# A language-model block on one core: shared down product with stationary weights, experts' first blocks fixed at the end, two gathers in flight

## Chip, cores and metric

One core of one Trainium2 chip. The metric is the device time of one execution, in microseconds, of this core.

## The reference

2048 tokens (4 sequences of 512) of width 128. Three steps, of which the third is the one that the change touches:

```python
h = take(W.T, x)                                       # embedding rows, 2048 x 128
h = h + ssm_attention(layernorm(h))                    # s = tanh(s @ A.T + x_t @ B.T), gated, projected
x = layernorm(h)
logits = x @ gate_w.T                                  # 8 experts, top 1
y = silu(x @ w1[e].T) * (x @ w3[e].T) @ w2[e].T        # e = the token's expert, inner width 512
y = y + gelu(x @ sw1.T) @ sw2.T                        # the shared expert, for every token
out = h + y
```

With one expert taken, its softmax weight is 1.

## The kernel before

**Until the experts.** The recurrence runs as 32 chunks of 16 steps side by side, with 40 steps of warm-up. Then each pair of 128-token tiles goes through gate, projection, second layernorm, transpose and router. The normed rows are also stored to DRAM (`x_rows`).

**The shared expert.** `up(n)` (16 units: group g = n // 4 of 512 tokens, inner chunk i = n % 4 of 128) makes a 512-column product for which ScalarE computes the gelu into `gelu_out[n]` (L792). Group 0 goes on in f32. For the other 12 units ScalarE makes an f16 high half (`act_high_half`, L797) and VectorE the f16 low half (`act_low_half`, L1096: both of its tensor inputs lie in SBUF). `down_part(n)` then multiplies by `sw2`. It has the activations stationary and 128 moving columns of weights: four matmuls for each of the four token tiles' sums in group 0 (L605), and in the others three f16 products (high*high, high*low, low*high) for each of four token tiles (L613). Each group's bank is first set by one product with zeros (L601). The result has tokens on partitions, so VectorE adds the bank to `attn_out` directly (`take_down(g)`, L1106, L1109) and SyncE stores it as the base of `out`.

**The index of the routed part.** VectorE works out from the router's one-hot matrix which slot of which block of 128 tokens each token goes to (L1131 to L1159), TensorE inverts this table (L629), and VectorE writes `row_in` and `row_of`, the row numbers of each block. 23 blocks would be enough for any routing. A flag `few_blocks` says whether 20 do; in this data they do, so 20 blocks run. The blocks stand in the order of the experts, so which expert a block has is data: TensorE loads it into a register (`load_expert`, L644) and addresses the weights by it.

**A block k.** GpSimd gathers its 128 rows from `x_rows` by an indirect DMA (`take_block`, L424). TensorE transposes them (`turn_block`, L639), ScalarE and VectorE split them into halves (`take_turned` L827, `turned_low` L1185). `block_ups` (L658) computes both up products, tokens on partitions, 2 x 3 matmuls of 512 columns. ScalarE: silu (L836). VectorE: product (L1207). TensorE transposes the product (L693, four). ScalarE and VectorE split it again (L843; L1220, which reads the transposed product in PSUM). TensorE: down product (L705, eight matmuls). VectorE: L1215 and L1234 put the two parts of it together in `out_blk[k % 8]`. GpSimd adds these rows to `out` in DRAM by an indirect DMA (`add_block`, L431).

**What sets the order.** Each engine runs its list in the order in which it is written, and semaphores tie the lists together. In step k of the pipeline TensorE has the ups of block k, the turn of block k+2, the transposes of block k-1 and the down product of block k-2. GpSimd's list is: 12 gathers, then eight times (add block k, gather block 12+k), then the other adds.

```python
for k in range(AHEAD):                                  # AHEAD = 12
    if k >= IN_FLIGHT:                                  # IN_FLIGHT = 3
        pool.wait_ge(xblk_in[k - IN_FLIGHT], 16)
    take_block(k)
...
for k in range(sure):                                   # sure = 15
    add_block(k)
    if AHEAD + k < FEW:                                 # FEW = 20
        take_block(AHEAD + k)
```

TensorE, ScalarE and VectorE read `few_blocks` into a register (`load_few`, L309) before the first step; TensorE does it after `down_part(11)`.

## Time and profile before

| what | value |
|---|---|
| median of 3 runs | 179.06 us (178.63 to 184.28) |
| the profiled execution | 178.78 us |
| its span in the trace | 177.0 us |
| TensorE, busy | 137.2 us (78%) |
| VectorE, busy | 125.1 us (71%) |
| ScalarE, busy | 102.5 us (58%) |
| GpSimd, busy | 83.8 us (47%) |

The span runs from the first to the last recorded event; 1.8 us of the execution's time lie outside it. Busy shares are averages over stages with different limits. Times within the trace are counted from the span's start.

### The profile page before, as it was taken

What the parts mean: (1) busy time and instruction counts of PE and PEld (TensorE: products, weight loads), DVE (VectorE), ACT (ScalarE), POOL (GpSimd) and SP (SyncE); (2) the same over time, 40 slices, a digit from 0 to 9 for tenths busy, and PEclk for the clock granted to TensorE, in tenths of its full rate; (3) what the DMA queues carried; (4) which work ended last, traced back from release to release, by engine and by line L of the source; (5) the groups of instructions that cost most, each with busy time, mean ns of one, the idle gap of its engine ahead of it and who ended that gap; (6) DMA issues with size and microseconds to landing.
All of it is one profiled execution on the core that took longest, in us unless ns stands there. A gap on an engine that the chain in (4) does not pass through costs nothing. (4 is left out here: it accounts for less than half of the span.)

```text
span 177.0 us, 3209 instructions
## 1 busy us (share of the span) xinstructions
PE 137.2 (78%) x989; PEld 100.6 (57%) x989; DVE 125.1 (71%) x362; ACT 102.5 (58%) x237; POOL 83.8 (47%) x77
## 2 busy tenths in 40 slices
PE   0104997778898888888599999879999999999510
PEld 0103875556666656677354698647667766666300
DVE  1245585947499985799968839668888888887610
ACT  2000454499989993476878993437565766564200
POOL 3767873910000000143300278740877778788760
PEclk9999999999999999999999999999999999999955
DMA  5565345999000000011110024150232244353340
GB/s 131 175 185 143 104 107 163 313 394 397 22 0 0 4 0 4 0 63 59 59 63 0 0 61 146 49 163 4 32 47 48 30 50 41 33 47 36 31 46 0
DMA packets 9955, 14.37 MB, mean 81 GB/s; under 512 B 1936, under 2 KB 4624, under 8 KB 9936
## 3 DMA queue, kind: packets, MB, share of 16 engines
q1 hardware_dynamic: 5904, 10.45, 17.2%
q0 software_dynamic: 4032, 3.67, 14.0%
q8 instruction: 11, 0.18, 0.4%
q14 instruction: 8, 0.07, 0.1%
HBM read 10.71 MB, written 3.41 MB: 80 GB/s over the span
## 5 line engine op out<-in xcount | busy, mean ns | idle before, releaser
L431 POOL DMA_INDIRECT out<-w_sb,row_of x20 | 31.4, 1572 | 11.9 <-DVE w_sb L1234 7.3
L484 PE MATMUL bank<-states,sq_sb 128*128 128x128 f32 x112 | 27.3, 327 | 6.5 <-ACT states L726 1.2
L658 PE MATMUL bank<-w_hl,xblk_t 128*128 x120 | 29.2, 379 | 0.3 <-issue 0.3
L412 POOL TENSOR_TENSOR rstd<-vareps,cst 128x2 f32<-128x2 f32 x8 | 5.7, 709 | 45.8 <-DVE vareps L877 45.8
L484 PEld LDWEIGHTS bank<-states,sq_sb 128*128 128x128 f32 x112 | 17.6, 198 | 15.0 <-ACT states L726 14.7
L482 PE MATMUL bank<-x_in,sq_sb 128*128 128x128 f32 x112 | 23.5, 292 | 1.6 <-ACT x_in L719 1.5
L726 ACT ACTIVATE states<-bank 128x128 f32<-128x128 f32 x56 | 15.5, 276 | 12.3 <-PE bank L484 12.1
L836 ACT ACTIVATE w_sb<-bank,factor 128x512 f32<-128x512 f32 x20 | 13.7, 687 | 13.0 <-PE bank L658 12.9
L424 POOL DMA_INDIRECT w_sb<-x_rows,row_in x16 | 18.0, 1122 | 4.9 <-issue 4.9
L482 PEld LDWEIGHTS bank<-x_in,sq_sb 128*128 128x128 f32 x112 | 18.1, 202 | 2.7 <-ACT x_in L719 1.6
L380 POOL DMA_INDIRECT emb_rows<-emb,tok_sb x16 | 15.6, 972 | 6.5 <-issue 4.3
L705 PE MATMUL bank<-w_hl,w_sb 128*128 x160 | 16.9, 249 | 2.0 <-DVE w_sb L1234 2.0
L1207 DVE SCALAR_TENSOR_TENSOR w_sb<-bank,factor,w_sb 128x512 f32<-128x512 f32 x20 | 15.0, 750 | 3.8 <-ACT w_sb L836 3.2
L658 PEld LDWEIGHTS bank<-w_hl,xblk_t 128*128 128x128 f16 x120 | 11.5, 98 | 10.2 <-issue 0.5
L705 PEld LDWEIGHTS bank<-w_hl,w_sb 128*128 128x128 f16 x160 | 13.1, 98 | 3.5 <-issue 2.5
L843 ACT ACTIVATE w_sb<-bank 128x512 f16<-128x512 f32 x20 | 11.9, 597 | 4.1 <-PE bank L693 4.1
L1220 DVE TENSOR_TENSOR w_sb<-bank,w_sb 128x512 f16<-128x512 f32 x20 | 13.6, 682 | 0.5 <-ACT w_sb L843 0.5
L693 PE MATMUL bank<-cst,w_sb 128*128 128x128 f32 x80 | 12.1, 273 | 0.0
L719 ACT ACTIVATE x_in<-bank 128x256 f32<-128x256 f32 x8 | 3.1, 387 | 14.9 <-PE bank L469 14.6
L1015 DVE SCALAR_TENSOR_TENSOR w_hl<-w_sb,scale_i,w_hl 128x512 f16<-128x512 f32 x16 | 11.1, 745 | 0.2
L542 PE MATMUL bank<-x_ffn,sw_hl 128*128 128x512 f16 x48 | 11.2, 379 | 0.0
L1215 DVE TENSOR_SCALAR out_part<-bank,factor 128x128 f32<-128x128 f32 x20 | 7.0, 351 | 5.5 <-PE bank L705 5.5
(162 smaller groups left out, 278.5 us busy)
## 6 DMA issues: line engine op xcount, KB each, us to landing
w_sb<-w SPq DMA_DIRECT2D x24, 256.0 KB, 5.8
x_rows<-norm SPq DMA_DIRECT2D x4, 256.0 KB, 2.4
out<-attn_out SPq DMA_DIRECT2D x4, 256.0 KB, 2.7
late<-places SPq DMA_DIRECT2D x1, 619.5 KB, 7.0
sw_sb<-sw SPq DMA_DIRECT2D x2, 256.0 KB, 2.9
cst<-consts SPq DMA_DIRECT2D x1, 420.0 KB, 3.8
sq_sb<-sq SPq DMA_DIRECT2D x1, 384.0 KB, 3.9
out<-w_sb,row_of POOLq DMA_INDIRECT x20, 3.4
```

Of the source, the lines that this page charges most:

```text
L380: pool.indirect_dma_start(out=emb_rows[:, t, :], out_offset=None, in_=emb, in_offset=bass.IndirectOffsetOnAxis(ap=tok_sb[:, t:t + 1], axis=0),
L424: pool.indirect_dma_start(out=xblk(k), out_offset=None, in_=x_rows, in_offset=bass.IndirectOffsetOnAxis(ap=row_in[:, k:k + 1], axis=0),).t ...
L431: pool.indirect_dma_start(out=out, out_offset=bass.IndirectOffsetOnAxis(ap=row_of[:, k:k + 1], axis=0), in_=out_blk[k % OUTS], in_offset=N ...
L482: pe.matmul(by_batch(pre), bt, x_at[:, p, :, PADK - shift:XB - shift], start=True, stop=False)
L484: pe.matmul(pre, at, states[:, i * COLS:(i + 1) * COLS], start=False, stop=True).then_inc(pre_ready, 1)
L658: mm = pe.matmul(hb[:], xblk_t[:, k % 3, b * P:(b + 1) * P], w[:, bass.ds(e * INNER + a * EXPERTS * INNER, INNER)], start=(j == 0), stop=( ...
L693: mm = pe.transpose(turned[1 - u][:, i * P:(i + 1) * P], prod[:, 1 - u, i * P:(i + 1) * P], ident)
L705: mm = pe.matmul(bank[6][:, 0:width], (prod_hi, prod_lo)[a][:, u, i * P:(i + 1) * P], w[:, bass.ds(at_i, width)], start=(i == 0 and a == 0 ...
L726: act.activation(states[:, (i + 1) * COLS:(i + 2) * COLS], bank[i % 2][:, 0:COLS], ACT.Tanh).then_inc(state_ready, 1)
L836: act.activation(silu[:, u, :], bank[u][:], ACT.Silu, scale=silu_in).then_inc(silu_ready, 1)
L1207: dve.scalar_tensor_tensor(out=prod[:, u, :], in0=bank[2 + u][:], scalar=prod_scale, in1=silu[:, u, :], op0=ALU.mult, op1=ALU.mult).then_i ...
L1220: dve.tensor_tensor(prod_lo[:, 1 - u, :], turned[1 - u][:], prod_hi[:, 1 - u, :], ALU.subtract).then_inc(prod_low, 1)
```

## The change

- `down_part` has the weights stationary and 512 moving token columns: 4 f32 matmuls for group 0, and 12 f16 ones for each other group. The product with zeros goes. The result now has the tokens on the columns, so ScalarE copies each bank to SBUF (`bring_base`), TensorE transposes it back in four pieces (`turn_base`), and VectorE adds the bank as before. The unscaling moves from VectorE's add to ScalarE's copy.
- Every expert gets at least one block. Each expert's first block has a fixed place, positions 12 to 19 (`own_expert`); the other blocks take positions 0 to 11 and 20 to 22. The index tables are laid out as 8 first blocks and 15 others, and `column(k)` says which column position k reads.
- A block with a fixed expert needs no register. Its ups have the weights stationary (24 matmuls of 128 columns), so the product comes out already transposed: the four transposes and their wait go, ScalarE and VectorE split the product from SBUF, the down product is 12 matmuls of 128 columns into one sum, and VectorE writes `out_blk` with one instruction where it had two.
- `load_few` stands behind step 21 on TensorE, ScalarE and VectorE, and three gathers in flight become two. GpSimd's list is otherwise as before: 12 gathers, then eight pairs, then adds.

```diff
-IN_FLIGHT = 3
+IN_FLIGHT = 2
+TURN_BASE = (5, 9, 13)
+BASE_OUT = (10, 15)
+SPREAD = BLOCKS - EXPERTS
+OWN_FROM = FEW - EXPERTS
...
+            for k in range(FEW + lag):
+                body(k, 0, FEW)
+            few = load_few(eng)
+            with eng.If(few == 0):
+                for k in range(FEW - 2, BLOCKS + lag):
+                    body(k, FEW, BLOCKS)
...
-                if i == 0:
-                    pe.matmul(down_bank[g][:], zeros[:], zeros[:, 0:1].to_broadcast([P, GC]), start=True, stop=False)
...
-                    for t in range(4):
-                        mm = pe.matmul(down_bank[g][:, t * P:(t + 1) * P], gelu_out[n][:, t * P:(t + 1) * P],
-                                       sw2_sb[:, i * P:(i + 1) * P], start=False, stop=(i == IC - 1 and t == 3))
...
+                    mm = pe.matmul(down_bank[g][:], sw2_sb[:, weights], gelu_out[n], start=(i == 0), stop=(i == IC - 1))
...
+                        mm = pe.matmul(down_bank[g][:], sw2_hl[:, b, weights], (act_hi, act_lo)[a][:, g, i, :],
+                                       start=(i == 0 and j == 0), stop=(i == IC - 1 and j == 2))
...
+            def turn_base(g):
+                pe.wait_ge(base_out, g + 1)
+                for t in range(4):
+                    mm = pe.transpose(down_bank[g][:, t * P:(t + 1) * P], base_cols[g][:, t * P:(t + 1) * P], ident)
+                mm.then_inc(base_turned, 1)
...
+                    if own is not None:
+                        for i in range(IC):
+                            at_i = own * INNER + i * P
+                            for j, (a, b) in enumerate(halves):
+                                mm = pe.matmul(hb[:, i * P:(i + 1) * P], w_hl[:, a, at_i:at_i + P],
+                                               xblk_t[:, k % 3, b * P:(b + 1) * P], start=(j == 0), stop=(j == 2))
...
+            def bring_base(g):
+                act.wait_ge(down_done, g + 1)
+                if g < WHOLE // IC:
+                    ins = act.activation(base_cols[g], down_bank[g][:], ACT.Copy)
...
+                if n - GELU_LEAD + WHOLE in BASE_OUT:
+                    bring_base(BASE_OUT.index(n - GELU_LEAD + WHOLE))
...
+                if k == 0:
+                    bring_base(GROUPS - 1)
...
             act.activation(table_probe[:], half_bg[0:1, 0:1], ACT.Silu)
+            bring_base(2)
             take_turned(1)
...
-            then_wait(dve.tensor_tensor(nth_hot[:], nths, lane_nth[:, 1:2, :].to_broadcast([P, BLOCKS, TILES]),
+            then_wait(dve.tensor_tensor(nth_hot[:], nth_of[:].unsqueeze(2).to_broadcast([P, BLOCKS, TILES]), lane_nth[:, 1:2, :].to_broadcast([P, BLOCKS, TILES]),
...
-                if n == 10:
+                if n == 11:
+                    take_down(0)
+                if n == 14:
                     take_down(1)
...
             take_down(2)
-            take_down(3)
...
+                if k == 0:
+                    take_down(3)
                 if live(-2):
                     turned_low(k + 2)
...
-                    dve.tensor_tensor(prod_lo[:, 1 - u, :], turned[1 - u][:], prod_hi[:, 1 - u, :], ALU.subtract
+                    full = turned[1 - u] if own_expert(k - 1) is None else prod[:, 1 - u, :]
+                    dve.tensor_tensor(prod_lo[:, 1 - u, :], full[:], prod_hi[:, 1 - u, :], ALU.subtract
```

Three places of the order matter to what follows. The first is ScalarE's list from the last gelu to the silu of block 1 (`states`, `x_in`, `emb_rows` and `w_sb` are the SBUF areas that gelu outputs, halves and base columns lie in). Before:

```order
L792 ACTIVATE w_sb<-bank,factor 128x512 [waits up_done]
L797 ACTIVATE states<-states,factor 128x512 [waits gelu_done] x3
L797 ACTIVATE states<-w_sb,factor 128x512 [waits gelu_done] x2
L827 ACTIVATE xblk_t<-bank 128x128 [waits blk_turned]
L846 ACT_TABLE_LOAD
L846 ACTIVATE table_probe<-half_bg 1x1
L827 ACTIVATE xblk_t<-bank 128x128 [waits blk_turned]
L309 TENSOR_LOAD few_blocks [waits experts_ready]
L309 ISA x2
L836 ACTIVATE w_sb<-bank,factor 128x512 [waits h_done]
L827 ACTIVATE xblk_t<-bank 128x128 [waits blk_turned]
```

And after:

```order
L849 ACTIVATE x_in<-bank 128x512 [waits down_done]
L839 ACTIVATE w_sb<-bank,factor 128x512 [waits up_done]
L844 ACTIVATE states<-states,factor 128x512 [waits gelu_done] x3
L844 ACTIVATE states<-w_sb,factor 128x512 [waits gelu_done] x2
L851 ACTIVATE emb_rows<-bank,factor 128x512 [waits down_done]
L884 ACTIVATE xblk_t<-bank 128x128 [waits blk_turned]
L910 ACT_TABLE_LOAD
L910 ACTIVATE table_probe<-half_bg 1x1
L851 ACTIVATE states<-bank,factor 128x512 [waits down_done]
L884 ACTIVATE xblk_t<-bank 128x128 [waits blk_turned]
L893 ACTIVATE w_sb<-bank,factor 128x512 [waits h_done]
L851 ACTIVATE states<-bank,factor 128x512 [waits down_done]
```

The four copies L849 and L851 stand between the conversions and the first blocks' work, each behind a wait for a finished bank; the load of the flag is gone from here.

The second is VectorE's list from the last low half to the first steps. Before:

```order
L1109 SCALAR_TENSOR_TENSOR attn_out<-bank,factor,attn_out 128x512 [waits down_done] x2
L309 TENSOR_LOAD few_blocks [waits experts_ready]
L309 ISA x2
L1207 SCALAR_TENSOR_TENSOR w_sb<-bank,factor,w_sb 128x512 [waits h_done,silu_ready]
L1185 TENSOR_TENSOR xblk_t<-bank,xblk_t 128x128 [waits xt_high]
```

And after:

```order
L1169 TENSOR_TENSOR attn_out<-bank,attn_out 128x512 [waits base_turned]
L1269 SCALAR_TENSOR_TENSOR w_sb<-bank,factor,w_sb 128x512 [waits h_done,silu_ready]
L1169 TENSOR_TENSOR attn_out<-bank,attn_out 128x512 [waits base_turned]
L1244 TENSOR_TENSOR xblk_t<-bank,xblk_t 128x128 [waits xt_high]
```

The last group's add now stands between the product of block 0 and the low half of block 2, and waits for transposes that TensorE does behind the ups of block 1.

The third is TensorE's list for one late step, the ups and turn of a block and the down product of the block two before. Before (with the transposes of the block between):

```order
L658 MATMUL bank<-w_hl,xblk_t 128x512 x2
L658 REGISTER_ALU
L658 MATMUL bank<-w_hl,xblk_t 128x512
L644 TENSOR_LOAD block_expert
L639 MATMUL bank<-cst,w_sb 128x128 [waits xt_ready,xblk_in16]
L693 MATMUL bank<-cst,w_sb 128x128 [waits prod_low,prod_ready]
L693 MATMUL bank<-cst,w_sb 128x128 x3
L705 ISA [waits outb_ready,prod_low]
L705 MATMUL bank<-w_hl,w_sb 128x256
```

And after:

```order
L682 MATMUL bank<-xblk_t,w_hl 128x128 [waits prod_ready,xt_ready]
L682 MATMUL bank<-xblk_t,w_hl 128x128 x23
L659 MATMUL bank<-cst,w_sb 128x128 [waits xt_ready,xblk_in17]
L738 MATMUL bank<-w_hl,w_sb 128x128 [waits prod_low]
L738 MATMUL bank<-w_hl,w_sb 128x128 x11
```

The four transposes L693 and the register load are gone from it.

## Rows read from the trace of the kernel before

**Rows 1.** Timeline of GpSimd (start us, length us, instruction, idle before): adds and a gather
```profile
123.57 1.62 POOL L431 DMA_INDIRECT out<-w_sb,row_of  x1 [5.86 <-DVE w_sb L1234]
125.49 0.99 POOL L424 DMA_INDIRECT w_sb<-x_rows,row_in  x1 [0.30 <-issue]
...
149.10 1.59 POOL L431 DMA_INDIRECT out<-w_sb,row_of  x1 [0.30 <-issue]
...
167.74 1.55 POOL L431 DMA_INDIRECT out<-w_sb,row_of  x1 [0.30 <-issue]
169.86 1.55 POOL L431 DMA_INDIRECT out<-w_sb,row_of  x1 [0.57 <-DVE w_sb L1234]
```
**Rows 2.** Timeline of VectorE: first and last finished output block
```profile
122.38 0.34 DVE L1234 SCALAR_TENSOR_TENSOR w_sb<-bank,factor,out_part 128x128 f32<-128x128 f32 x1
...
169.23 0.35 DVE L1234 SCALAR_TENSOR_TENSOR w_sb<-bank,factor,out_part 128x128 f32<-128x128 f32 x1
```
**Rows 3.** Timeline of TensorE: one step of the steady pipeline
```profile
150.66 0.82 PE L705 MATMUL bank<-w_hl,w_sb 128*128 x8
...
151.32 1.46 PE L658 MATMUL bank<-w_hl,xblk_t 128*128 x6
152.62 0.27 PE L639 MATMUL bank<-cst,w_sb 128*128 128x128 f32 x1
152.72 0.60 PE L693 MATMUL bank<-cst,w_sb 128*128 128x128 f32 x4
153.16 0.82 PE L705 MATMUL bank<-w_hl,w_sb 128*128 x8
```
**Rows 4.** Timeline of TensorE: shared down product and the first blocks
```profile
98.21 1.20 PE L629 MATMUL bank<-nth_row,w_sb 128*128 128x23 f16 x16
...
100.54 0.38 PE L601 MATMUL bank<-zeros 128*128 128x512 f16 x1
100.75 3.73 PE L605 MATMUL bank<-sw_sb,x_in 128*128 128x128 f32 x32
104.32 0.38 PE L601 MATMUL bank<-zeros 128*128 128x512 f16 x1
...
107.22 0.38 PE L601 MATMUL bank<-zeros 128*128 128x512 f16 x1
...
111.27 0.38 PE L601 MATMUL bank<-zeros 128*128 128x512 f16 x1 [0.87 <-issue]
...
118.81 1.46 PE L658 MATMUL bank<-w_hl,xblk_t 128*128 x6
```
**Rows 5.** Timeline of VectorE: index chain, and its first step
```profile
96.28 0.35 DVE L1156 TENSOR_TENSOR nth_hot<-late,lane_nth 128x368 f16<-128x368 f16 x1
...
96.93 1.22 DVE L1159 TENSOR_TENSOR w_sb<-late,lane_nth 128x2048 f16<-128x2048 f16 x1
...
117.11 0.75 DVE L1207 SCALAR_TENSOR_TENSOR w_sb<-bank,factor,w_sb 128x512 f32<-128x512 f32 x1 [0.59 <-PE bank L658]
```
**Rows 6.** Timeline of ScalarE: last conversions, table load
```profile
105.68 1.35 ACT L797 ACTIVATE states<-w_sb,factor 128x512 f16<-128x512 f32 x2
...
110.06 1.28 ACT L846 ACT_TABLE_LOAD   x1
```
**Rows 7.** Timelines: a gather beside a low half, a gather beside none, that low half
```profile
114.06 1.16 POOL L424 DMA_INDIRECT w_sb<-x_rows,row_in  x1 [0.30 <-issue]
115.52 0.94 POOL L424 DMA_INDIRECT w_sb<-x_rows,row_in  x1 [0.30 <-issue]
...
113.66 0.74 DVE L1096 SCALAR_TENSOR_TENSOR w_sb<-w_sb,factor,states 128x512 f16<-128x512 f32 x1
```
**Rows 8.** Groups by line and shape, VectorE's index chain: busy, mean ns
```profile
L1145 DVE TENSOR_REDUCE slot_f<-place_own 128x16 f32<-128x128 f32 x1 | 0.4, 376 | 0.0
...
L1163 DVE TENSOR_SCALAR row_in<-bank 128x23 int32<-128x23 f32 x1 | 0.2, 181 | 0.6 <-PE bank L629 0.6
```
**Rows 9.** DMA to landing of all GpSimd gathers (source line L424)
```profile
DMA to landing us min/median/max: 2.5/2.7/4.6
```

More of the change, by code:

```diff
@@ L240, in build @@
                     + [w1_sb[:, i * GC:(i + 1) * GC] for i in range(2)])
+        base_cols = [gelu_out[g * IC] for g in range(GROUPS)]
         table_probe = sb("table_probe", [1, 1])
-        zeros = sb("zeros", [P, P], F16)
         lane_hot = w1_sb[:, 2 * INNER:2 * INNER + TILES * P // 2].bitcast(F16).rearrange("q (p t) -> q p t", t=TILES)
@@ L309, in load_few, with pipelined @@
             return eng.value_load(few_blocks[0:1, 0:1], min_val=0, max_val=1)
-        def pipelined(eng, body, lag, few):
-            for k in range(FEW - 2):
-                body(k, k % RING, k, BLOCKS)
-            for is_few, end in ((0, BLOCKS), (1, FEW)):
-                with eng.If(few == is_few):
-                    for k in range(FEW - 2, end + lag):
-                        body(k, k % RING, k, end)
+        def pipelined(eng, body, lag):
+            for k in range(FEW + lag):
[4 more added lines that the diff above has]
+                    body(k, FEW, BLOCKS)
         def pair_tiles(n):
@@ L667, in _ @@
                 if n == TURN_FIRST + 1:
-                    few = load_few(pe)
                     load_expert(0, 0)
                     load_expert(1, 1)
+                if n in TURN_BASE:
+                    turn_base(TURN_BASE.index(n))
                 if n == TURN_SECOND:
@@ L675, in _, with step @@
             block_ups(1)
-            def step(k, v, static, end):
-                live = lambda d: static is None or 0 <= static - d < end
-                u = v % 2
+            turn_base(GROUPS - 1)
+            def step(k, first, end):
+                live = lambda d: first <= k - d < end
+                u = k % 2
                 if live(0) and k >= 2:
                     block_ups(k)
-                if live(-1) and k >= 1:
-                    load_expert(k + 1, (v + 1) % RING)
+                if live(-1) and k >= 1 and own_expert(k + 1) is None:
+                    load_expert(k + 1, (k + 1) % RING)
                 if live(-2):
                     turn_block(k + 2)
-                if live(1):
+                if live(1) and own_expert(k - 1) is None:
                     pe.wait_ge(prod_ready, k)
-                    if k >= 3:
+                    if k >= 3 and own_expert(k - 3) is not None:
+                        pe.wait_ge(outb_ready, k - 2)
+                    elif k >= 3:
                         pe.wait_ge(prod_low, k - 2)
@@ L694, in step @@
                     mm.then_inc(prod_turned, 1)
-                if live(2):
-                    e2 = pe.snap(expert_of[(v - 2) % RING], min_val=0, max_val=EXPERTS - 1)
+                if live(2) and own_expert(k - 2) is not None:
+                    own = own_expert(k - 2)
                     pe.wait_ge(prod_low, k - 1)
-                    if static is None or static >= 3:
+                    if k >= 4 and own_expert(k - 4) is not None:
+                        pe.wait_ge(outb_ready, k - 3)
+                    elif k < 4:
+                        pe.wait_ge(base_ready, k + 1)
+                    for i in range(IC):
+                        for j, (a, b) in enumerate(((0, 0), (1, 0), (0, 1)) if i == 0 else ((1, 0), (0, 1), (0, 0))):
+                            mm = pe.matmul(turned[u][:, 0:P], (prod_hi, prod_lo)[a][:, u, i * P:(i + 1) * P],
+                                           w2_hl[:, own * IC + i, b, :],
+                                           start=(i == 0 and j == 0), stop=(i == IC - 1 and j == 2))
+                    mm.then_inc(y_done, 1)
+                elif live(2):
+                    e2 = pe.snap(expert_of[(k - 2) % RING], min_val=0, max_val=EXPERTS - 1)
+                    pe.wait_ge(prod_low, k - 1)
+                    if k >= 3:
                         pe.wait_ge(outb_ready, k - 2)
@@ L708, in step @@
                     mm.then_inc(y_done, 1)
-            pipelined(pe, step, 2, few)
+            pipelined(pe, step, 2)
         @block.scalar
@@ L1196, in _, with step @@
             take_down(2)
-            take_down(3)
-            def step(k, v, static, end):
-                live = lambda d: static is None or 0 <= static - d < end
-                u = v % 2
+            def step(k, first, end):
+                live = lambda d: first <= k - d < end
+                u = k % 2
                 if live(0):
```

129 lines of the change are left out of this document (74 added, 55 removed).

## The prediction

> **What bounds the kernel now.** I read the timeline of GpSimd from the back first. The last add of a block starts at 169.86 [rows 1], and the span ends 7.1 us later (177.0), when it has landed. Before it GpSimd ran without a rest. From the first add (123.57) to the ninth (149.10) it alternates add and gather: 25.53 us for eight pairs, 3.19 each. From there to the nineteenth (167.74) there are only adds, 18.64 us for ten, 1.86 each, with 0.30 idle put down to "issue" [rows 1]. Those two prices hold whatever TensorE does. Then I read VectorE: the first output block is done at 122.72 and the last at 169.58 [rows 2]. TensorE's step is 2.50 us, 150.66 to 153.16 [rows 3]. So for eight blocks GpSimd falls back (3.19 against 2.50, 5.5 us behind) and then catches up 0.64 a block; at the twentieth it has just caught up: it waited 0.27 us more than usual (0.57 against 0.30). Had every block been ready early, the last add would have started at 123.57 + 25.53 + 11 x 1.864 = 169.60. TensorE's path puts it at 169.86. The routed part has two bounds 0.3 us apart, and both hang on when the first output block is finished. TensorE's 78% and GpSimd's 47% of the page do not show this; GpSimd's 47% is a mean over a span in which it hardly works before 100 us.
>
> What comes ahead of the first block is one chain: VectorE's index chain releases TensorE's inversion (VectorE ends 98.15, TensorE starts 98.21) [rows 4, 5], the last up products follow, and from 100.54 TensorE does the shared down product and the ups of blocks 0 and 1. The ups of block 2 start at 118.81 [rows 4], and the first output is finished 3.91 us later.
>
> **The change, part by part.**
>
> *Own experts' steps.* The ups are 24 products of 128 columns where six of 512 stood. The f16 quarter of the shared product is such work: 48 products of 128 columns in 2.90 us less 0.22 for the zeros [rows 4], 0.056 each. So the ups take 1.34 against 1.30, the down product 12 x 0.056 = 0.67 against 0.66, the turn 0.10, and the transposes' 0.44 goes [rows 3]. A step is 2.11 instead of 2.50. Eight of them save 3.1 us of TensorE, and the drain at the end is shorter, since product, split and down product follow without a transpose; from the ups' end to the last output I count 3.5 us less 0.6 of slack, some 2 us better than now. TensorE alone would gain 5 us against the first block. What is late next is GpSimd, whose list is the same. It cannot start its last add before the first add's start + 46.03 (25.53 + 11 x 1.864). So of this gain 0.3 us could be seen, and nothing more.
>
> *Index chain.* Four VectorE instructions are added ahead of `nth_hot` (96.28 [rows 5]), set between the chain's own so that they add their length and no wait: a compare of 120 elements, a reduction of 120, an add of 15, a copy of 8. Nearest rows: the reduction of 128 took 0.376 [rows 8], a small one 0.181. In a row, instructions overlap by about 0.08, and so I take 0.21 + 0.28 + 0.09 + 0.08 = 0.65. `nth_hot` (368 f16 elements) now reads one input that repeats each element 16 times. Now it takes 0.35 [rows 5]. At the rate of the f16-and-f32 low half (0.74 for 512 against 0.18 for 23, 0.00115 us an element) [rows 7, 8] it would be 0.57. I take 0.10 for it, between 0 and 0.22, and 0.75 in all; ends 0.4 and 1.1. It hides behind nothing: TensorE's inversion started 0.06 us after this chain. TensorE's shared part starts at 101.3.
>
> The Trainium skill, "VectorE: DVE Perf Modes", section on what auto-detection checks, says that the fast 16-bit mode is taken only where every tensor has a step of plus or minus one. A repeated element has step 0. By that rule the whole 0.22 is paid and the sum is 0.12 higher; that 2048 elements took 1.22 [rows 5], well under the slow rate, agrees that the mode is in use today.
>
> *Shared down product, by itself.* Group 0: 32 passes of 128 columns in 3.57 us (100.75 to 104.32), 0.112 each; four products of 512 columns are eight passes of four times that less what the loads cost. Bounds: 0.9 x and 1.0 x, so 3.2 to 3.6; I take 3.4, against 3.78 with the zeros. The other groups: 12 products of 512 columns at 0.216 (six in 1.30 [rows 3]) = 2.6 against 2.9. Together 1.3 us less. The four times four transposes add 4 x 0.44 = 1.8. TensorE's own work rises by 0.5 us.
>
> *The round trip over ScalarE.* Here the order decides. I write the new times down, at 0.62 for each 512-column ScalarE copy (two in 1.35 [rows 6], 0.07 of it the last one's tail) and 0.15 for TensorE to start after a wait.
> - Group 0 is done at 104.85. ScalarE is free from 103.3 (105.68 [rows 6] less three conversions and a gelu) and its list has the copy ahead of the last gelu: it waits 1.6 us, copies until 105.5, and then has the gelu and five conversions, 3.7 us: 109.2 instead of 107.0.
> - The second copy follows, 109.2 to 109.9. TensorE comes to its transposes at 109.0 (quarters of 0.65, first transposes 0.45), waits 1.0 and goes on at 110.5.
> - Unit 10, the turn of block 0 (111.1), unit 11. ScalarE takes block 0 over, loads the table (1.28 [rows 6]) and only then copies bank 2: 113.1 to 113.8. TensorE transposes it at 114.0, turns block 1 at 114.4 and does the ups of block 0 from 114.5, units 14 and 15 from 115.8, the ups of block 1 from 117.1, and at 118.4 the last transposes.
> - VectorE's add of the last group waits for these until 119.1, though block 0's product is long done, and behind it in its list stands the low half of block 2 (to 120.0). TensorE turns block 3 then, does four transposes and starts the ups of block 2 at 120.7.
>
> Against this, reading the flag is gone from here: 0.87 idle on TensorE [rows 4] and 0.59 on VectorE [rows 5]. The two expert loads stay; I take 0.5 us for them, and the wait for the copies covers most. 120.7 against 118.81 is 1.9 us later. Bounds: 1.3, if the index chain costs its least, the register loads nothing and the copies 0.55; 2.8, if the chain costs its most and loads keep their whole 0.87.
>
> *Two gathers in flight.* A gather lands 2.7 us after its start in the median [rows 9]. Two in flight give 1.35 us a gather against the 1.25 of GpSimd's own work (0.94 + 0.30), so twelve end near 118 to 121, before the first add. Nothing then hangs on it. Bound: at 4.6 [rows 9] each the twelfth starts at 101.2 + 5 x 4.6 + 1.3 = 125.5, and the first add comes 1.9 later still.
>
> *Collision on own steps.* VectorE's low half reads product and high half both from SBUF in these steps. The trace shows what such an instruction does to GpSimd: the low half at 113.66 ran to 114.40, the gather started at 114.06 took 1.16, a gather free of any took 0.94 [rows 7]. It looks as if it stood until the other's end. An add that starts inside such a stretch of 0.65 us loses up to 0.65. Three other gathers show the pattern, starting inside low halves; two that had started ahead of one lost next to nothing. With the phases above I get 0.1 us in all, and up to 1.6 if they shift by 0.4; I take 0.2. Lower end 0.
>
> The Trainium skill, "SBUF — State Buffer", section "Who interferes with whom", says that a VectorE instruction with two SBUF inputs contends with a GpSimd instruction that reads SBUF, and the one that comes second stands still. It speaks against this change; the slow gathers agree with it. By it the first rival below is more likely than the trace alone makes it.
>
> **The sum**, against the profiled execution: first add 123.57 + 1.9 = 125.5; last add 125.5 + 46.0 + 0.2 = 171.7; end of the span 171.7 + 7.1 = 178.8; with the 1.8 us outside it, 180.6. That execution took 178.78 and the median is 179.06, so this is 0.9% over the median.
>
> **Rivals.**
> - *Lock-step of adds and low halves (slower).* Once an add starts inside a low half and stands to its end, the next starts 1.86 later while the low half's end comes 2.11 later, so it is inside again. GpSimd then runs at 2.11 or worse in the own steps, and where an add meets one twice it loses 0.4 on average. 8 x 0.25 to 8 x 0.65 = 2 to 5 us; at 0.4 each 3.2, which gives 180.4 + 3.2 = 183.6. It decides from 2.2 us on. For it: the slow gathers. Against: adds are not gathers, and no row shows an add beside such an instruction.
> - *The start-up delay is hidden.* If the index chain and the first copy cost little and the flag loads were worth more than I count, the first add starts near 123.6 and the time is 178.8. For it: 0.87 + 0.59 us of flag loads go. Against: the copies stand in ScalarE's list before conversions on which TensorE waits.
> - *GpSimd isn't a bound.* If its adds run faster when nothing is queued, the matrix path decides: last output at 124.6 + 46.86 - 5 = 166.5, end of the span 166.5 + 0.3 + 7.1 = 173.9, time 175.7. Against: ten adds in a row at 1.86 with no wait on a block.
> - *Gathers late.* First add at 127.4, time 182.4. For it: one landing of 4.6. Against: the median of 2.7.
>
> **Chances.** Forecast 0.62, lock-step 0.12, hidden delay 0.16, GpSimd no bound 0.04, late gathers 0.06. The range goes from 178.8 (hidden delay) to 182.6 (upper bound of the start-up, the start of lock-step). A change of 2% (3.6 us) is about what a measurement of this kernel can tell from none. Faster than 175.5 needs the third rival and a little more: 0.02. Slower than 182.6 needs most of lock-step's cases: 0.10. Within 2%: 0.88.
>
> **What would show it.** First add near 125.4, and from there eight pairs at 3.2 and adds at 1.86 with 0.30 idle to the end; TensorE's late steps at 2.11 and its last product at least 4 us before the last add starts; ScalarE idle before its first bank copy and TensorE before the second transposes; VectorE idle some 2 us before the last group's add. Wrong if the first add starts before 124, if adds take visibly longer than 1.55 in the late part, or if GpSimd waits for blocks at the end.

## The result and the profile after

| kernel | median of 12 runs, same chip | profiled execution | its span |
|---|---|---|---|
| before | 179.39 us (178.01 to 186.66) | 178.78 us | 177.0 us |
| changed | 181.69 us (180.13 to 187.17) | 180.32 us | 178.2 us |

The ratio changed / before is 1.0102, 95% interval 1.0065 to 1.0139. The change costs 1.0%: more than no difference, less than 2%. The forecast was 180.6 us against a profiled execution of 178.78 us, the same 1.0%; the median of the changed kernel, 181.69 us, lies 1.1 us above it.

The page of the changed kernel, its head and its chain that ended last:

```profile
span 178.2 us, 3155 instructions
...
PE 134.4 (75%) x1013; PEld 97.8 (55%) x1013; DVE 121.8 (68%) x355; ACT 104.5 (59%) x241; POOL 82.1 (46%) x77
...
POOL 2%; issue 0%
POOL out L451 2%
```

TensorE is 2.8 us less busy, VectorE 3.3, and the time went up. The chain that the page gives is short, the last two adds of GpSimd and the 0.3 us before each. GpSimd's timeline (start, length, instruction, idle before and what ended it):

```profile
100.91 1.02 POOL L444 DMA_INDIRECT xblk<-x_rows,row_in  x1 [13.78 <-DVE row_in L1227]
...
111.37 0.94 POOL L444 DMA_INDIRECT w_sb<-x_rows,row_in  x1 [1.71 <-DMA w_sb<-x_rows,row_in]
...
119.04 0.94 POOL L444 DMA_INDIRECT w_sb<-x_rows,row_in  x1 [0.51 <-DMA w_sb<-x_rows,row_in]
124.88 1.62 POOL L451 DMA_INDIRECT out<-w_sb,row_of  x1 [4.90 <-DVE w_sb L1301]
...
150.41 1.59 POOL L451 DMA_INDIRECT out<-w_sb,row_of  x1 [0.31 <-issue]
...
169.04 1.55 POOL L451 DMA_INDIRECT out<-w_sb,row_of  x1 [0.30 <-issue]
170.90 1.55 POOL L451 DMA_INDIRECT out<-w_sb,row_of  x1 [0.30 <-issue]
```

The pattern of [rows 1] is there again: eight pairs in 25.53 us (124.88 to 150.41), then single adds 1.86 apart. But where the last add waited 0.57 for VectorE, it now has the plain 0.30: it waits for no block. From the first to the last add it is 46.02 us, before 46.29.

TensorE and VectorE in the last steps:

```profile
152.13 1.50 PE L682 MATMUL bank<-xblk_t,w_hl 128*128 128x128 f16 x24
153.47 0.28 PE L659 MATMUL bank<-cst,w_sb 128*128 128x128 f32 x1
153.59 0.83 PE L738 MATMUL bank<-w_hl,w_sb 128*128 128x128 f16 x12
154.26 1.50 PE L682 MATMUL bank<-xblk_t,w_hl 128*128 128x128 f16 x24
...
163.53 1.70 PE L738 MATMUL bank<-w_hl,w_sb 128*128 128x128 f16 x24 [0.83 <-DVE w_sb L1285]
...
165.34 0.35 DVE L1305 TENSOR_SCALAR w_sb<-bank,factor 128x128 f32<-128x128 f32 x1 [0.51 <-PE bank L738]
```

The step is 2.13 us (152.13 to 154.26) where [rows 3] has 2.50, and the last output block is finished at 165.69, before at 169.58 [rows 2]. The matrix path (TensorE, ScalarE and VectorE up to the finished output block) ends 3.9 us earlier, and the last block lies ready for 5.2 us when its add starts. From first to last output block it takes 41.66 us (124.03 to 165.69), before 46.86 (122.72 to 169.58), so 5.2 less.

The start, on VectorE, ScalarE and TensorE:

```profile
96.54 0.54 DVE L1220 TENSOR_TENSOR nth_hot<-nth_of,lane_nth 128x368 f16<-128x368 f16 x1
...
97.38 1.22 DVE L1223 TENSOR_TENSOR w_sb<-late,lane_nth 128x2048 f16<-128x2048 f16 x1
...
118.50 0.69 DVE L1169 TENSOR_TENSOR attn_out<-bank,attn_out 128x512 f32<-128x512 f32 x1 [1.80 <-PE bank L635]
119.11 0.28 DVE L1244 TENSOR_TENSOR xblk_t<-bank,xblk_t 128x128 f16<-128x128 f32 x1
...
104.66 0.60 ACT L849 ACTIVATE x_in<-bank 128x512 f32<-128x512 f32 x1 [1.54 <-PE bank L623]
...
101.03 3.60 PE L623 MATMUL bank<-x_in,sw_sb 128*128 128x512 f32 x8
...
109.51 0.66 PE L635 MATMUL bank<-cst,emb_rows 128*128 128x128 f32 x4 [0.57 <-ACT emb_rows L851]
...
119.54 0.30 PE L659 MATMUL bank<-cst,xblk 128*128 128x128 f32 x1 [0.96 <-DVE xblk_t L1244]
...
120.12 1.24 PE L688 MATMUL bank<-w_hl,xblk_t 128*128 x5
```

From the end of the index chain to the ups of block 2 it is 98.60 to 120.12 = 21.52 us, before 98.15 to 118.81 = 20.66 [rows 4, 5]. The last group's add (118.50) waits 1.80 for its transposes, the low half of block 2 stands behind it, and TensorE waits 0.96 for that. The first add starts 1.31 us later than before (124.88 against 123.57). Everything behind it is a list that keeps this delay. Of the delay the change itself makes 1.60: 0.86 in this stretch and 0.74 in the index chain; the chain started 0.29 earlier in this trace.

In the experiments a stretch is counted within its trace, from the start of the first gather, because that gather starts anywhere from 99.65 to 107.04 us in the traces, whatever the edit behind it. So the index chain, which lies ahead of it, is left out of these stretches. In the kernel before the first gather starts at 100.43:

```profile
100.43 1.02 POOL L424 DMA_INDIRECT xblk<-x_rows,row_in  x1 [13.01 <-DVE row_in L1163]
```

So it has 23.14 us from first gather to first add and 69.43 to the last; the changed kernel has 23.97 and 69.99. Two more traces of kernels with the changed kernel's order up to the first add repeat its 23.97 (23.97 and 23.98, below). The profiled execution of the changed kernel with the old down product had a mean granted clock of 0.937 but 1.00 from its first gather to its first add, so its stretches are used and its time is told by its ratio alone.

### The profile page after: what moved, and what is told of

Its sections match the earlier page's. It is cut to its first block and busy times, and to the rows that moved or that the text cites. A ratio compares the mean times of both kernels' runs of the same rounds, so it can differ in the third digit from the quotient of the medians.

```text
span 178.2 us, 3155 instructions
## 1 busy us (share of the span) xinstructions
PE 134.4 (75%) x1013; PEld 97.8 (55%) x1013; DVE 121.8 (68%) x355; ACT 104.5 (59%) x241; POOL 82.1 (46%) x77
## 5 line engine op out<-in xcount | busy, mean ns | idle before, releaser
L444 POOL DMA_INDIRECT w_sb<-x_rows,row_in x16 | 15.6, 974 | 8.2 <-DMA w_sb<-x_rows,row_in 4.2
L688 PE MATMUL bank<-w_hl,xblk_t 128*128 x72 | 17.5, 379 | 0.0
L682 PE MATMUL bank<-xblk_t,w_hl 128*128 128x128 f16 x192 | 12.0, 219 | 0.0
L444 POOL DMA_INDIRECT xblk<-x_rows,row_in x4 | 4.6, 1145 | 14.9 <-DVE row_in L1227 13.8
L682 PEld LDWEIGHTS bank<-xblk_t,w_hl 128*128 128x128 f16 x192 | 11.2, 98 | 0.0
L796 ACT ACTIVATE attn_out<-w_sb 128x512 f32<-128x512 f32 x16 | 10.0, 625 | 0.9 <-DMA w_sb<-w 0.5
L688 PEld LDWEIGHTS bank<-w_hl,xblk_t 128*128 128x128 f16 x72 | 6.9, 98 | 6.1
L489 PE MATMUL bank<-cst,norm_rows 128*128 128x128 f32 x16 | 4.1, 345 | 8.1 <-DVE norm_rows L945 8.0
L752 PE MATMUL bank<-w_hl,w_sb 128*128 x96 | 9.9, 246 | 0.0
```

The lines of the kernel that those rows point to most:

```text
L444: pool.indirect_dma_start(out=xblk(k), out_offset=None, in_=x_rows, in_offset=bass.IndirectOffsetOnAxis(ap=row_in[:, column(k):column(k) + ...
L682: mm = pe.matmul(hb[:, i * P:(i + 1) * P], w_hl[:, a, at_i:at_i + P], xblk_t[:, k % 3, b * P:(b + 1) * P], start=(j == 0), stop=(j == 2))
L688: mm = pe.matmul(hb[:], xblk_t[:, k % 3, b * P:(b + 1) * P], w[:, bass.ds(e * INNER + a * EXPERTS * INNER, INNER)], start=(j == 0), stop=( ...
```

## The experiments

**Which of the two bounds holds? 16 gathers ahead.** The GpSimd list then has four pairs and fifteen adds: 4 x 3.19 + 15 x 1.86 = 40.7 us instead of 46.0.

```diff
-AHEAD = 12
+AHEAD = 16
```

On the changed kernel:

> The changed kernel with 16 gathers ahead of the first add where it had 12, so that four of the gathers (1.29 us each) leave the stretch behind the first add. Theory (GpSimd's own list sets the end): the 16 gathers at about 1.5 us each end near 126, the first add starts near 126.3 instead of 124.9, then four pairs of 3.19 and fifteen adds of 1.86, last add near 167.0 instead of 170.9, time near 176.4 (the changed kernel's profiled run had 180.3). Rival (TensorE's blocks set the end): nothing is won, 180 to 182.

Measured: 181.83 us median, ratio to the kernel before 1.0094 (1.0043 to 1.0145; all ratios below are to the kernel before, too). The forecast gain didn't come.

```profile
127.78 0.94 POOL L444 DMA_INDIRECT w_sb<-x_rows,row_in  x1 [3.61 <-DMA w_sb<-x_rows,row_in]
...
130.61 0.94 POOL L444 DMA_INDIRECT w_sb<-x_rows,row_in  x1 [0.64 <-DMA w_sb<-x_rows,row_in]
132.02 1.62 POOL L451 DMA_INDIRECT out<-w_sb,row_of  x1 [0.46 <-issue]
...
172.73 1.55 POOL L451 DMA_INDIRECT out<-w_sb,row_of  x1 [0.30 <-issue]
```

The list is 40.71 us long, as worked out, with no wait on a block: GpSimd's list is the bound. But with two in flight the 16 gathers last until 131.55, where the forecast had 126. One landing alone costs 3.61 us of idle time, and the first add comes 29.22 us after the first gather (102.80). The list is 5.3 us shorter and starts 5.25 us later.

On the kernel before:

> The kernel before with 16 gathers ahead where it had 12. Theory (TensorE's list and GpSimd's were 0.3 us apart there): the adds no longer follow each other without a wait, yet the last one starts where it did (169.9), because the last block is finished only at 169.6: same time, within 0.3 us of 178.8. Rival (GpSimd alone was the bound): as much is won as in the changed kernel, 3.5 to 5 us, 174 to 175.

Measured: 179.67 us, ratio 1.0007 (0.9949 to 1.0064).

```profile
122.99 1.62 POOL L431 DMA_INDIRECT out<-w_sb,row_of  x1 [0.46 <-issue]
...
149.71 1.55 POOL L431 DMA_INDIRECT out<-w_sb,row_of  x1 [0.95 <-DVE w_sb L1234]
...
162.92 1.55 POOL L431 DMA_INDIRECT out<-w_sb,row_of  x1 [1.65 <-DVE w_sb L1234]
...
169.14 1.55 POOL L431 DMA_INDIRECT out<-w_sb,row_of  x1 [0.30 <-DVE w_sb L1234]
```

With three in flight the gathers are out of the way in time (first add 23.34 us after the first gather). The list is shorter, and the adds now wait for VectorE's output; the last add starts 69.49 us after the first gather, with 12 ahead 69.43. Both bounds of the prediction are seen: in the kernel before, the matrix path and the list end together; in the changed kernel the matrix path ends 5.2 us ahead of the last add.

**Which part makes the start late?** The kernel before with the new shared down product alone (new `down_part`, `bring_base`, `turn_base`, their places; index and flag loads as before):

```diff
+                    mm = pe.matmul(down_bank[g][:], sw2_sb[:, weights], gelu_out[n], start=(i == 0), stop=(i == IC - 1))
...
+                if n in TURN_BASE:
+                    turn_base(TURN_BASE.index(n))
```

> The kernel before with the shared down product of the change alone (stationary weights, copies by ScalarE, transposes); index chain, blocks and flag loads as before. Theory (the round trip over ScalarE costs about 0.6 to 1.2 us, and the end follows the first add): first add 0.6 to 1.2 us later than 123.6, last add later by the same, time 179.4 to 180.0. Rival (512 moving columns pay for the transposes): first add not later, 178.5 or less.

Measured: 181.46 us, ratio 1.0056 (1.0004 to 1.0108). First gather 101.72, first add:

```profile
125.83 1.62 POOL L434 DMA_INDIRECT out<-w_sb,row_of  x1 [7.52 <-DVE w_sb L1246]
```

That is 24.11 us, 0.97 more than before, inside the forecast of 0.6 to 1.2. The last add waits 0.96 for its block here and starts 70.78 us after the first gather, 1.35 more than before: this kernel still has the steps of the old blocks, and the matrix path ends last.

The changed kernel with the old down product:

```diff
-                    mm = pe.matmul(down_bank[g][:], sw2_sb[:, weights], gelu_out[n], start=(i == 0), stop=(i == IC - 1))
...
-                if n in TURN_BASE:
-                    turn_base(TURN_BASE.index(n))
```

> The changed kernel with the shared down product of before (zeros, 128 moving columns, no copies, no transposes). Theory: the index chain's 0.74 is left, the flag loads' 0.9 on TensorE and 0.6 on VectorE are gone, so that the first add starts at 123.0 to 123.6 and the last 46.0 later, at 169.0 to 169.6: time 178.0 to 178.7, some 2 us under the changed kernel, though TensorE's last product is then some 6 us ahead of the last add. Rival (the shared down product is not what delays the first add): 180 to 181, as the changed kernel.

Measured: 179.54 us, ratio 0.9992 (0.9943 to 1.0041). First gather 105.35, first add:

```profile
115.16 0.38 PE L622 MATMUL bank<-zeros 128*128 128x512 f16 x1
...
127.17 1.62 POOL L452 DMA_INDIRECT out<-w_sb,row_of  x1 [2.23 <-DVE w_sb L1293]
...
173.19 1.55 POOL L452 DMA_INDIRECT out<-w_sb,row_of  x1 [0.30 <-issue]
```

That is 21.82 us to the first add, and 46.02 for the list. Four kernels give the table of the start, us from first gather to first add:

| | old down product | new down product | difference |
|---|---|---|---|
| flag loaded before the first step | 23.14 (before) | 24.11 | +0.97 |
| flag loaded behind step 21 | 21.82 | 23.97 (changed) | +2.15 |
| difference | -1.32 | -0.14 | |

The rows of the table differ in the flag loads, and also in the index tables, in the late blocks and in the number in flight; no run moved the flag loads alone. What else the traces show agrees with putting the difference down to them. The number in flight is nothing here (below), and the late blocks come behind the first add. In the left column 1.03 of the 1.32 us lie at TensorE's next product with zeros (L601 before, L622 here), which had 0.87 idle ahead of it in [rows 4] and has none here, and 0.29 in the wait before the turn of block 3 (1.07 before, 0.78 here).

So moving the flag loads is worth 1.32 us with the old down product and almost nothing with the new one. Why they cost nothing there is not shown: with the new down product TensorE's products on both sides of that place start 0.44 us apart with the flag load between them (112.64 and 113.08) and without it (111.84 and 112.28), and neither waits for a bank copy. The new down product costs 2.15 us at the start of this kernel. Without it the changed kernel is level with the one before, in spite of the dearer index chain (0.74), and the two intervals (0.9943 to 1.0041 against 1.0065 to 1.0139) lie apart.

**The last group's round trip, moved.** The changed kernel with the last transposes and the last add behind those of block 2:

```diff
-            turn_base(GROUPS - 1)
...
+                if k == 0:
+                    turn_base(GROUPS - 1)
...
                 if live(-2):
                     turned_low(k + 2)
+                if k == 0:
+                    take_down(3)
```

(On TensorE they stand behind `turn_block` of step 0.)

> The changed kernel with the last group's four base transposes moved on TensorE behind the transpose of block 2 in step 0, and VectorE's add of the last base moved behind the low half of block 2. Theory A (the GpSimd list begins when the first output block is there, and its end follows one for one; the last group's round trip stands ahead of that block): the first add comes 0.5 to 1.0 us earlier, 23.0 to 23.5 us after the first gather instead of 23.97, the last add 46.02 us later than that, time 180.7 to 181.2 us against the changed kernel's 181.7, ratio 1.004 to 1.009. Theory B (block 2's own chain, its ups and SiLU, decides the first output block, and the last group's round trip hides beside it): first add where it was, 23.9 to 24.0 us after the first gather, ratio 1.008 to 1.012.

Measured: 180.55 us, ratio 1.0053 (1.0007 to 1.0099). First gather 102.00:

```profile
125.36 1.62 POOL L451 DMA_INDIRECT out<-w_sb,row_of  x1 [4.28 <-DVE w_sb L1302]
...
171.37 1.55 POOL L451 DMA_INDIRECT out<-w_sb,row_of  x1 [0.30 <-issue]
```

First add 23.36 us behind, so 0.61 earlier than in the changed kernel, and the list 46.01 behind it. Theory A holds in the trace: one wait in the order is worth 0.6 us, and the end follows it. The times alone don't tell the two kernels apart, since this interval overlaps with the changed kernel's (1.0065 to 1.0139).

**Two or three in flight.** The kernel before with two:

```diff
-IN_FLIGHT = 3
+IN_FLIGHT = 2
```

> The kernel before with IN_FLIGHT = 2 and nothing else. Theory A (on an undisturbed chip the number in flight is nothing): the first add stays where TensorE's path puts it, some 23.1 us after the first gather, the adds begin 46.0 to 46.3 us apart from first to last, and the time is that of the kernel before, ratio 0.99 to 1.01; the waits on landings that two in flight bring (0.5 to 1.7 us each in the changed kernel) end before the first add. Theory B (three in flight is what lengthens the start of the adds on some chips, where the kernel before takes near 189 us): if the kernel before takes over 185 us on this chip, this one is 2 to 4% faster than it; if the kernel before takes near 179 us, B says the same as A. Theory C (ten adds later the third gather in flight was needed): the gathers end over 2 us later and the first add with them, +1 to +2 us.

Measured: 179.58 us, ratio 0.9979 (0.9924 to 1.0035). The first gather starts at 101.30 and the first add at 124.45, 23.15 later, before 23.14. From the first to the last add it is 46.96, outside the forecast of 46.0 to 46.3: the last add waits for a block, as before, and VectorE's outputs come later at one step, 3.22 apart where the kernel before has 2.85 and the kernel before with 16 ahead 3.20. That is the step at which the engines of the kernel before branch on `few_blocks`; the steps ahead of it take 2.50.

The changed kernel with three:

```diff
-IN_FLIGHT = 2
+IN_FLIGHT = 3
```

> The changed kernel with IN_FLIGHT = 3. On the chip where the kernel before took 189 us this kernel's first add came 28.1 us after its first gather, after a stretch in which ScalarE and TensorE sat idle for 2 to 6 us and no engine's work released them. Theory A (that stretch belongs to a chip, not to the kernel): on a chip where the kernel before takes near 179 us, the first add comes 23.9 to 24.1 us after the first gather, as with two in flight, and the time is the changed kernel's own, 181 to 182 us, ratio 1.005 to 1.015. Theory B (three in flight with the new down product makes the stretch on every chip): the first add comes 26 us or more after the first gather and the time is 184 to 188.

Measured: 182.19 us, ratio 1.0117 (1.0058 to 1.0175). From 102.43 to 126.41 it is 23.98, with two 23.97. With 12 gathers ahead the number in flight changes nothing at the first add. With 16 the gathers of the changed kernel end 28.8 us after the first one's start with two in flight, and 21.5 with three (104.88 to 126.40, in a run of the other occasion below).

**A low half beside an add: the rival that didn't come.** The changed kernel with one more VectorE instruction in each step from 12 to 19, whose two inputs lie in SBUF and whose output nobody reads:

```diff
+                if 12 <= k < FEW:
+                    dve.tensor_tensor(junk, cst[:, C_IDENT + 128:C_IDENT + 128 + INNER], cst[:, 0:INNER], ALU.add)
```

> The changed kernel with one more VectorE instruction in each of steps 12 to 19: a 128x512 f32 sum of two SBUF inputs into an unused area (0.7 us, its result is not used), so that in the late steps VectorE has two SBUF inputs for about 1.3 of every 2.4 us while GpSimd makes its adds without a rest. Theory (a GpSimd indirect DMA that starts beside such an instruction stands until it ends): some of the adds behind step 12 show 1.7 to 2.3 us where they now show 1.55, and the last add starts 1 to 4 us later. Rival (only gathers, or nothing, is held up): all at 1.55 and a last add 46.0 behind the first.

Measured: 185.53 us in one run, on the occasion on which the kernel before took 189.41 (see below), so it has no ratio and is read from its trace alone. GpSimd's adds, and three of VectorE's instructions (L1290 is the added one, L1286 the low half that is there anyway):

```profile
159.23 2.01 POOL L452 DMA_INDIRECT out<-w_sb,row_of  x1 [0.30 <-issue]
161.55 2.01 POOL L452 DMA_INDIRECT out<-w_sb,row_of  x1 [0.31 <-issue]
163.87 2.02 POOL L452 DMA_INDIRECT out<-w_sb,row_of  x1 [0.30 <-issue]
166.19 2.01 POOL L452 DMA_INDIRECT out<-w_sb,row_of  x1 [0.30 <-issue]
...
159.14 0.68 DVE L1286 TENSOR_TENSOR w_sb<-w_sb 128x512 f16<-128x512 f32 x1
...
160.86 0.68 DVE L1290 TENSOR_TENSOR w_sb<-cst 128x512 f32<-128x512 f32 x1
161.46 0.68 DVE L1286 TENSOR_TENSOR w_sb<-w_sb 128x512 f16<-128x512 f32 x1
```

An add that takes 1.55 takes 2.01 where it starts 0.09 us into a low half (159.23 against 159.14, 161.55 against 161.46). The added instructions don't hold it up by themselves: L1290 at 160.86 runs beside an add that had started before it. What they do is make VectorE's step longer. From add to add it is now 2.32 us, which is VectorE's own step (159.14 to 161.46), though no add waits for a block: GpSimd and VectorE go in lock-step for four adds. The last add comes 48.57 us after the first, 2.55 more than in the changed kernel. The first comes 23.97 us after the first gather, as there. In the changed kernel itself the adds beside the own steps took 1.55 to 1.57, so its collision cost was nothing. But it was near: its adds started 0.99, 0.72, 0.46, 0.19 and 0.14 us after the end of a low half, and the next one (163.46) 0.01 before an end (163.47). The low halves of the steps come closer by the difference of the two periods, 2.13 against 1.86, and the own steps ended before they met.

**The best combination.** Old down product, 16 ahead, three in flight, on the changed kernel (the edits above together):

> The changed kernel with the old shared down product, 16 gathers ahead and three in flight. Theory A (the GpSimd list is the bound of the changed kernel, and on an undisturbed chip gathers put ahead take it away): from the chain's end to the first output block 24.1 us as in the changed kernel with the old down product, list of 40.7 us instead of 46.0, so that TensorE's path decides the end, shortened by the eight own steps (2.11 instead of 2.50 us) and the shorter drain: last add 4 to 5 us earlier than in the changed kernel, 175.5 to 177.5 us in time, ratio 0.98 to 0.99. Theory B (the adds cannot start before the gathers of 16 are down, and with them the start moves by 5 us or the adds wait for blocks): last add where it was, 179 to 181 us, ratio 0.995 to 1.005. If the kernel before takes near 189 us on this chip, neither can be told.

Measured: 178.11 us (4 runs), ratio 0.9863 (0.9765 to 0.9961): faster than before by 1.4%, with an interval from 0.4% to 2.4%, and the lowest ratio of all. First gather 101.52.

```profile
122.15 0.34 DVE L1293 SCALAR_TENSOR_TENSOR w_sb<-bank,factor,out_part 128x128 f32<-128x128 f32 x1
...
122.27 0.94 POOL L445 DMA_INDIRECT w_sb<-x_rows,row_in  x1 [1.99 <-DMA w_sb<-x_rows,row_in]
...
125.12 0.95 POOL L445 DMA_INDIRECT w_sb<-x_rows,row_in  x1 [0.30 <-DVE w_sb L1293]
126.37 1.62 POOL L452 DMA_INDIRECT out<-w_sb,row_of  x1 [0.30 <-issue]
...
161.64 1.70 POOL L452 DMA_INDIRECT out<-w_sb,row_of  x1 [0.30 <-issue]
...
161.24 0.68 DVE L1277 TENSOR_TENSOR w_sb<-w_sb 128x512 f16<-128x512 f32 x1
...
163.79 0.35 DVE L1297 TENSOR_SCALAR w_sb<-bank,factor 128x128 f32<-128x128 f32 x1 [0.51 <-PE bank L738]
...
167.37 1.55 POOL L452 DMA_INDIRECT out<-w_sb,row_of  x1 [0.30 <-issue]
```

The first output block is ready at 122.49, but the gathers last until 126.07, so the adds begin 3.9 us after they could. The last one starts 65.85 us after the first gather, 4.1 less than in the changed kernel. Of this 2.15 is the old down product (69.99 to 67.84, the changed kernel with the old down product alone) and 2.0 the gathers. VectorE was done at 164.14, so GpSimd is still the bound. Theory A had the gain in the trace right and its place wrong: the matrix path was not reached. The median missed its 175.5 to 177.5 us. The list takes 41.00 us instead of 40.71, since here some adds do start inside low halves: the one at 161.64 (low half 161.24 to 161.92) takes 1.70. Whether a number between 12 and 16 ahead is better was not tried.

**The same kernels on another occasion.** Three kernels had been run earlier on the same chip, on an occasion when the kernel before took 189.41 us median (188.04 to 191.62, 7 runs), against 180.33 later: the changed kernel with 16 ahead and three in flight, the changed kernel with three in flight, and the best combination. In this order:

> The changed kernel with 16 gathers ahead and three in flight. Counted from the end of VectorE's index chain (98.60 in the changed kernel's trace, where its last add starts 72.3 later). Theory: three in flight end the 16 gathers some 25 after it, the first add starts at 26.3 as in the changed kernel, the rest of GpSimd's list is four pairs of 3.19 and fifteen adds of 1.86 = 40.7 instead of 46.0, so its bound is 67.0; the last block is finished at 67.1, and the last add starts at 67.4: time near 175.4, 4.9 under the changed kernel, and adds that wait for blocks at the end. Rival (the first run of this kind missed because the list length is not the bound): 180 to 182 again.

> The changed kernel with three gathers in flight, twelve ahead as it has. Theory (the twelve gathers end 5 us before the first add and nothing hangs on them): first add 26.3 after the index chain, last add 46.0 after that, time as the changed kernel, 180 to 181. Rival (two in flight is part of the loss): first add earlier than 25.8, time 179.5 or less.

> The changed kernel's experts' blocks and flag loads, with the shared down product of before, 16 gathers ahead and three in flight. Theory: blocks could start their adds 24.1 after the index chain, but the 16 gathers end at 25.2 (as in the kernel before with 16 ahead), first add 25.6, last add 40.7 later at 66.3, the last block finished at 64.9: 6.0 under the changed kernel, time near 174.3, 0.973 of the kernel before. Rival (the down product's transposes cost nothing once GpSimd is relieved): same as the run with the new down product, 175.4.

Measured: 190.06 (ratio 0.9947, 0.9871 to 1.0024), 187.5 (no ratio), and 193.29 us (1.019, 1.0105 to 1.0275). From first gather to first add 33.4, 28.1 and 34.0 us. ScalarE in the second and third of these:

```profile
118.80 0.28 ACT L884 ACTIVATE xblk_t<-bank 128x128 f16<-128x128 f32 x1 [3.77 <-remote]
```

```profile
131.73 0.28 ACT L874 ACTIVATE xblk_t<-bank 128x128 f16<-128x128 f32 x1 [8.88 <-remote]
```

ScalarE stands for 3.77 and 8.88 us, and in the first of the three for 2.57 and 5.73, in the stretch of the gathers and of the bases' stores, and no work of this core ends the wait. These three are inconclusive about the edits: the identical kernel of the second gave 23.98 us later (above), that of the third 24.85. The kernel with the added instruction (two in flight) was run on that occasion too. In its one run no such wait stands ahead of the first add, but ScalarE stood 1.59 and 1.64 us in the same way at 151.86 and 155.07, before the adds read above. What held the engines, and whether more gathers in flight invite it, stays open.

## Why the prediction was right

- *Two bounds, 0.3 us apart, with the change moving only the one that isn't GpSimd's.* Right, and shown from both sides by 16 gathers ahead: the changed kernel waits for no block, the kernel before does. From first to last add 46.02 us, forecast 46.03 + 0.2. It also explains why so little of the saving shows: the matrix path is 5.2 us shorter against the first block (forecast 5), and from first to last add 0.27 of it can be seen. Not all of it is the own steps: one step of the kernel before took 2.85 instead of 2.50, the one with the branch on `few_blocks`, which the changed kernel has behind its blocks. The prediction did not count it, and no run has it alone.
- *Own steps.* 2.13 measured, 2.11 forecast.
- *Index chain.* 5.11 us before (93.04 to 98.15) and 5.85 after, +0.74; forecast 0.75. Inside it, `nth_hot` costs +0.19 (0.54 against 0.35) where I took 0.10, and the four added instructions 0.55 where I took 0.65: two errors that cancel by luck. No run has the new chain alone, but GpSimd's wait for `row_in` before the first gather agrees with the 0.74 in every trace: it is 13.01 to 13.05 us with the old chain, and 13.73 to 13.78 with the new one. The Trainium skill, "VectorE: DVE Perf Modes", section on what auto-detection checks, says that the fast 16-bit mode of a two-input instruction needs a step of plus or minus one in every tensor. This 0.54 agrees: with a repeated element the instruction ran at nearly the slow rate (0.57 by the prediction's rows).
- *Start-up delay, the term that was mis-sized.* Forecast 1.9, measured 1.31. The trace after reaches the start of the index chain 0.29 earlier (92.75 against 93.04), which is no part of the change, so the change's own delay is 1.60. The chain is right; the rest, from the chain's end to block 2's ups, was put at 1.15 and is 0.86. Inside that: the expert loads, put at 0.5, cost about 0.2 (TensorE's products at 111.84 and 112.28 start 0.44 apart, where such a product takes 0.22), and nothing with the old down product (115.10 and 115.16); the wait before the second transposes was 0.57 and not 1.0; the waits of ScalarE before its first copy (1.54 against 1.6) and of VectorE before the last group's add (1.80 against 2) are where I put them. Part by part, the new down product costs 2.15 and the flag loads give back 1.32. I had 0.87 and 0.59 as the rows' idle before them and never said what that is worth in the sum: with the old down product nearly all of it, with the new one 0.14.
- *Collision.* 0.2 forecast, 0 measured. The mechanism was real, and luck with the phases kept it away. With one more instruction a step, the lock-step rival appeared at 2.55 us, inside its forecast of 2 to 5. The Trainium skill, "SBUF — State Buffer", section "Who interferes with whom", says that a VectorE instruction with two SBUF inputs contends with a GpSimd instruction that reads SBUF, and these 2.01 us agree. The prediction had the add stand until the low half's end; measured, it loses 0.13 us less than that: 0.46 with 0.59 left of the low half (159.23), 0.15 with 0.28 left (161.64 in the best combination).
- *Two in flight.* Nothing, as forecast: 23.15 against 23.14 us, and 23.97 against 23.98 at the first add. A gather took more than the 1.35 us that I had (19.07 us for twelve), and there was room for it: twelve gathers ended at 119.98, inside the forecast of 118 to 121.
- *The end.* 170.90 to the span's end took 7.3 us (forecast 7.1), and 2.1 us lie outside the span (1.8). These 0.5 us and the 0.8 that the last add came sooner than forecast (171.7) nearly cancel, which is luck. So the 180.6 is nearer to 180.32 than its parts were.

## What to carry to other kernels

Where two engines' lists end within 0.3 us of each other, taking 0.4 us out of each step of one of them buys next to nothing. Read from the back which engine's last instructions run without a wait, and ask what sets its first one. A rearrangement that trades matmuls for a trip over another engine has to be priced by the waits in each in-order list. Two savings at the same place need not add up (the flag loads: 1.32 us with one down product, 0.14 with the other). Moving work ahead of a list's start (16 gathers) pays only if that work is done by then, which took three in flight here, and only where the list is the bound.

## What the runs showed that I had not expected

- The price of gathers ahead hangs on how many are in flight: 16 of them end 28.8 us after the first one's start in the changed kernel with two in flight (131.55 less 102.80). With three they take 21.5 in the changed kernel on the other occasion, 22.9 in the kernel before (122.52 less 99.65) and 24.6 in the best combination (126.07 less 101.52). GpSimd waited 3.61 us for a single landing where the median landing took 2.7 [rows 9].
- GpSimd and VectorE can lock: an add of 1.55 us became 2.01 in four steps running, and its period VectorE's 2.32.
- The same program on the same chip took 189.4 us on one occasion and 180.3 on another, and on the first ScalarE stood up to 8.88 us, in another kernel, with no releaser in this core. Ratios compare runs of one occasion for this reason.
